# Reordering the setup of a decoupled cross-attention kernel: mask counts, first transposes, image values, output weights and the second batch's keys

## The chip, the cores and the metric

The kernel runs on one core of a Trainium2 chip. The metric is device time in microseconds of one execution; lower is better. Engines are named as in the profile: PE is the matrix engine, PEld its weight loads, DVE the vector engine, ACT the scalar engine, POOL GpSimd, SP the engine that here only issues transfers. A name with q (SPq, ACTq) is an engine's issue of a transfer.

## The reference, cut to what matters

```python
q = split_heads(hidden_states @ w_q, 20)          # hidden_states: 2 x 2048 x 640
k = split_heads(text @ w_k, 20); v = split_heads(text @ w_v, 20)     # text: 2 x 146 x 1024
out_text = merge(sdpa(q, k, v))
mask_ip = ip_mask(bbox, ...)                      # 0 or -10000 for each query and image token
k_ip = split_heads(ip_h @ w_k_ip, 20); v_ip = split_heads(ip_h @ w_v_ip, 20)   # ip_h: 2 x 8 x 1024
out_ip = merge(sdpa(q, k_ip, v_ip, mask=mask_ip))
out = (out_text + out_ip) @ w_out + b_out + residual
```

Each of 20 heads of width 32 attends to 146 text keys and, with a softmax of its own, to 8 image keys.

## The kernel before, in words

Queries are worked in 16 blocks of 256. The first eight belong to batch 0. The work of a block is spread over three stages, of which three neighbouring blocks are in flight at a time: NEXT (X: the transposes of the next block's input), FRONT (Q: query products of five head groups; S: scores with queries on partitions, for their maxima) and BACK (AUX: the maxima transposed; ST: scores with keys on partitions, then the exponentials; PV; AT; O). Each engine walks a list written out by hand (`STEPS`, `ACT_STEPS`, `DVE_STEPS`, `SP_STEPS`), in its order, and waits on counters. Iteration t=0 has FRONT and NEXT only, t=1 is the first with all three.

Every float operand of the large products is split in a high and a low part: ACT copies the high part (`w_high`, `x_high`), DVE subtracts to get the low part (`w_low`, `x_low`), and value units get three parts by `split_values` (first the copy by ACT, then subtract, cast and subtract on DVE).

Before t=0 lies a setup. PE transposes the context, then makes the text keys in five groups (L901), one each as the key weights arrive. Between groups it makes eight "counts" (L913), products of a box indicator with 0/1 weights, which DVE turns into the mask (`mask_values`, L713), four for each batch, through one SBUF tile `mask`. ACT stores a finished half of the mask to DRAM (L572), and DVE's count number 4 waits until the first store has landed. DVE makes the indicator before (L688 to L696) and raises `s_msk` to 3 with it. After the groups come the image keys (L922, bank 7), their rearrangement by a second product (L932, after ACT's `k_ip_rows`), and the transposes of block 0's input (X, L980). The counter `s_klo` reaches 6 when all keys are done. SP then copies batch 0's keys to the stacked operand `k_stack` in 12 issues (`keys_to_stack`, L382), and for each block it copies the queries in two sets to `q_stack` (12 issues each at L457, one of the mask at L460); the first scores wait for both.

Values come in six units (`V_UNITS`, `make_values`): two for batch 0, the 18 remaining text keys of both batches ("rest"), the image tokens ("ip", L960, weights `w_v_ip`), and two for batch 1. They are placed among the steps of t=0 and t=1. Banks 5 to 7 serve them and the key groups; later they are the ST banks. In t=1, before ST(0,2), PE waits for the whole split of all four large units:

```python
if t == 1 and (kind, *args) == ("ST", 0, 2):
    pe.wait_ge(s_vsplit, 4 * V_PARTS)
```

The output weights `wo` are loaded by SP at the end of t=0 and split at five ST steps of t=1 (`W_O_PLACES`; L560 on ACT, L725 on DVE). POOL fills tiles at the start, then casts constant rows into `k_stack` (L490) and copies `v_tail` (L497).

Of the kernel before, what the change touches and what calls it, by code (L numbers as in the profile page):

```python
# [31 lines left out]
F32 = mybir.dt.float32  # L32
# [7 lines left out]
P = 128  # L40
# [28 lines left out]
W_Q_PLACES = {3: (0, 1), 4: (2, 3, 4)}  # L69
# [64 lines left out]
}  # L134
V_COPY_PLACES = {(0, "S", 0, 0, 0): (0, 1), (0, "S", 1, 0, 0): (2,), (0, "S", 1, 1, 0): (3,), (1, "Q", 1): (4,), (1, "ST", 0, 2): (5,)}
V_SPLIT_PLACES = {(0, "S", 0, 0, 0): (0, 1), (1, "S", 4, 0, 0): (4,), (1, "S", 4, 0, 1): (5,)}
W_O_PLACES = {("ST", 2, 0): 0, ("ST", 2, 1): 1, ("ST", 3, 0): 2, ("ST", 3, 1): 3, ("ST", 4, 0): 4}
COUNTS = {0: (0, 3), 1: (3, 4), 3: (4, 7), 4: (7, 8)}
# [83 lines left out]
def attention_kernel(nc, x, ctx, boxes, wq, wk, wv, wk_ip, wv_ip, wo, b_out,  # L222
# [5 lines left out]
    with ExitStack() as stack:  # L228
# [51 lines left out]
        inv_den = sb("inv_den", [P, QT, 8])  # L280
# [82 lines left out]
        def _(sp):  # L363
# [50 lines left out]
            def body(it):  # L414
                t = it.t
                if not it.back:

                    sp.wait_ge(s_klo, GROUPS + 1)

                    sp.wait_ge(stored, 16 * BATCHES)  # L420
                    keys_to_stack(0)
                for stage, kind, args, gen, sc in it.steps(SP_STEPS if it.back else SP_FIRST):
# [10 lines left out]
                    if kind == "XIN":  # L433
# [4 lines left out]
                        if not it.back:  # L438
                            sp.dma_start(w_v_ip, wv_ip.rearrange("(c p) n -> p c n", p=P)).then_inc(s_wv_ip, 16)
# [27 lines left out]
                if not it.back:  # L467
                    before_aux()
# [6 lines left out]
        def _(pool):  # L475
# [6 lines left out]
            nc.gpsimd.memset(k_ip_rows[:], 0.0).then_inc(s_ip_zero, 1)  # L482
            for b in range(BATCHES):
# [48 lines left out]
        def _(act):  # L532
# [29 lines left out]
            for g in range(GROUPS):  # L562
# [4 lines left out]
                                     ACT.Copy, scale=SCALE).then_inc(s_khi, 1)  # L567
                if g in (2, 4):
# [4 lines left out]
                for n in W_Q_PLACES.get(g, ()):  # L573
                    w_high(n)
            act.wait_ge(s_ip_zero, 1)
            act.wait_ge(s_kp, K_IP + 1)
            for j in range(4):
                rows = slice(32 * j, 32 * j + BATCHES * IP)
                nc.scalar.activation(k_ip_rows[rows, :, j, :], k_bank(K_IP)[rows, 0:GROUPS * DH].rearrange("p (g d) -> p g d", d=DH),
                                     ACT.Copy).then_inc(s_ip_rows, 1)  # L580
            act.wait_ge(s_kp, K_IP_T + 1)
            for b in range(BATCHES):
                nc.scalar.activation(k_hi[:, :, b, TEXT:CTX],
                                     k_bank(K_IP_T)[:, 0:GROUPS * BATCHES * IP].rearrange("p (g b k) -> p g b k", g=GROUPS, b=BATCHES)[:, :, b, :],
                                     ACT.Copy, scale=SCALE).then_inc(s_khi, 1)
# [35 lines left out]

            def body(it):
# [47 lines left out]
        def _(dve):  # L670
# [33 lines left out]
            def mask_values(first, end):  # L704

                for n in range(first, end):
# [6 lines left out]
                    nc.vector.tensor_scalar(mask[:, 512 * c:512 * (c + 1)], bank[2 + n % 3][0:IP, :], -1.0, -NEG,  # L713
# [26 lines left out]
            dve.wait_ge(s_khi, GROUPS + BATCHES)  # L740
            for b in range(BATCHES):
                last = nc.vector.scalar_tensor_tensor(
                    out=k_lo[:, :, b, TEXT:CTX],
                    in0=k_bank(K_IP_T)[:, 0:GROUPS * BATCHES * IP].rearrange("p (g b k) -> p g b k", g=GROUPS, b=BATCHES)[:, :, b, :],
                    scalar=SCALE, in1=k_hi[:, :, b, TEXT:CTX].bitcast(F32), op0=ALU.mult, op1=ALU.subtract)
            last.then_inc(s_klo, 1)

# [31 lines left out]

            def body(it):  # L780
# [4 lines left out]
                for stage, kind, args, gen, sc in it.steps(DVE_STEPS):  # L785
                    if isinstance(t, int) and t == 1 and (kind, *args) in W_O_PLACES:
# [86 lines left out]
        def _(pe):  # L873
# [18 lines left out]
            for g in range(GROUPS):  # L892
# [11 lines left out]
                for n in range(*COUNTS.get(g, (0, 0))):  # L904
# [5 lines left out]
                    if n >= 3:  # L910

                        pe.wait_ge(s_mval, n - 2)
                    nc.tensor.matmul(bank[2 + n % 3][0:IP, :], pick[0:9, IP * b:IP * (b + 1)],  # L913
                                     inside[:, 512 * c:512 * (c + 1)], start=True, stop=True).then_inc(s_cnt, 1)

            pe.wait_ge(s_ctx_t, BATCHES + 2)
            pe.wait_ge(s_wk_ip, 16)
            pe.wait_ge(s_klo, 3)
            heads = w_k_ip[:].rearrange("p c (g j d) -> p c g j d", j=4, d=DH)
            for c in range(CC):  # L920
                for j in range(4):
                    last = nc.tensor.matmul(k_bank(K_IP)[32 * j:32 * j + BATCHES * IP, 0:GROUPS * DH],  # L922
# [297 lines left out]
```

## Time and profile before

| | |
|---|---|
| time, median of 3 | 734.93 us (734.69 to 735.64) |
| profiled execution, its own time | 729.49 us |
| its span | 727.7 us |
| PE busy over the span | 688.1 us (95%) |
| DVE, ACT, POOL busy | 74%, 40%, 29% |

The span runs from the first to the last instruction; the execution's own time is 1.8 us longer. Times in rows count from the span's start. In a timeline a row is a run of equal instructions: start, length, engine, line, operation, tiles, and in brackets the engine's idle time before it and what ended it.

### The profile page before, as it was taken

What the parts mean: (1) busy time and instruction counts of PE and PEld (TensorE: products, weight loads), DVE (VectorE), ACT (ScalarE), POOL (GpSimd) and SP (SyncE); (2) the same over time, 40 slices, a digit from 0 to 9 for tenths busy, and PEclk for the clock granted to TensorE, in tenths of its full rate; (3) what the DMA queues carried; (4) which work ended last, traced back from release to release, by engine and by line L of the source; (5) the groups of instructions that cost most, each with busy time, mean ns of one, the idle gap of its engine ahead of it and who ended that gap; (6) DMA issues with size and microseconds to landing.
All of it is one profiled execution on the core that took longest, in us unless ns stands there. A gap on an engine that the chain in (4) does not pass through costs nothing.

```text
span 727.7 us, 18922 instructions
## 1 busy us (share of the span) xinstructions
PE 688.1 (95%) x6410; PEld 628.2 (86%) x6410; DVE 540.1 (74%) x1686; ACT 288.3 (40%) x626; POOL 213.5 (29%) x359
## 2 busy tenths in 40 slices
PE   4979778999999999999999999999999999999987
PEld 3567467989999998989999999999999989899876
DVE  5341539878787979797878788787879797978764
ACT  1031117153534435261617162535444261617061
POOL 7100004324150504142423324151505042423223
PEclk9879999999999999999999999999999999999979
DMA  9935954253434444433435263534344444434310
GB/s 266 323 98 137 267 147 121 66 155 92 136 90 134 102 127 103 140 89 102 130 89 156 68 163 82 147 96 127 98 127 103 133 96 125 104 92 114 90 49 37
DMA packets 79543, 89.52 MB, mean 123 GB/s; under 512 B 10680, under 2 KB 63416, under 8 KB 79492
## 3 DMA queue, kind: packets, MB, share of 16 engines
q1 hardware_dynamic: 79016, 88.45, 44.7%
q10 hardware_dynamic: 492, 0.61, 0.4%
q8 instruction: 21, 0.34, 0.2%
q14 instruction: 14, 0.11, 0.1%
HBM read 39.21 MB, written 10.62 MB: 68 GB/s over the span
## 4 chain that ended last, share of the span: by engine, by line
PE 75%; DMA 8%; DVE 7%; SPq 6%; issue 2%; ACT 1%; ACTq 0%; POOL 0%; DVEq 0%
PE psum L1019 32%; PE psum L1124 9%; PE psum L1076 7%; PE psum L1108 6%; PE psum L1103 5%; DMA q_stack<-aux_a 4%; SPq L457 3%; PE psum L1132 3%; PE psum L901 3%; PE psum L1133 2%; SPq L429 2%; DMA wo_raw<-in_L_xattn_w_v_ip 2%; PE psum L1147 2%; PE psum L980 2%; PE psum L1130 1%
## 5 line engine op out<-in xcount | busy, mean ns | idle before, releaser
L522 POOL TENSOR_TENSOR attn<-o_parts 128x128 f32<-128x128 f32 x160 | 73.8, 461 | 418.9 <-DVE o_parts L844 418.9
L803 DVE TENSOR_REDUCE neg_max<-psum 128x2 f32<-128x292 f32 x320 | 144.7, 452 | 64.0 <-PE psum L1076 63.4
L1019 PE MATMUL psum<-wo_both,at_hi 128*128 128x320 f32 x640 | 153.2, 313 | 0.0
L1019 PE MATMUL psum<-xt_hi,wq_hi 128*128 128x256 f32 x400 | 114.9, 287 | 1.4 <-DVE xt_lo L773 1.4
L1076 PE MATMUL psum<-k_stack,q_stack 104*128 104x154 f32 x640 | 112.6, 286 | 3.5 <-DVE neg_max L804 1.5
L1019 PE MATMUL psum<-xt_hi,wq_lo 128*128 128x256 f32 x400 | 112.1, 280 | 0.0
L1019 PE MATMUL psum<-xt_lo,wq_hi 128*128 128x256 f32 x400 | 112.0, 280 | 0.0
L831 DVE TENSOR_TENSOR p_lo<-psum,p_hi 128x512 f16<-128x512 f32 x160 | 107.9, 682 | 2.8 <-ACT psum L657 2.8
L1019 PEld LDWEIGHTS psum<-wo_both,at_hi 128*128 128x128 f32 x640 | 109.6, 188 | 0.0
L655 ACT ACTIVATE p_hi<-psum 128x512 f16<-128x512 f32 x160 | 95.3, 595 | 27.8 <-PE psum L1103 27.7
L1124 PE MATMUL psum<-v_tail,p_tail 128*128 128x264 f32 x320 | 102.0, 400 | 2.6 <-DVE p_lo L831 1.6
L1076 PEld LDWEIGHTS psum<-k_stack,q_stack 104*128 104x128 f32 x640 | 89.7, 192 | 13.0 <-DVE neg_max L804 9.1
L1019 PE MATMUL psum<-wo_both,at_lo 128*128 128x320 f32 x320 | 98.7, 308 | 0.0
L657 ACT ACTIVATE psum<-psum 128x512 f32<-128x512 f32 x160 | 96.6, 603 | 0.0
L646 ACT ACTIVATE q_hi<-psum 128x256 fp32r<-128x256 f32 x80 | 31.0, 387 | 140.8 <-PE psum L1019 140.8
L527 POOL TENSOR_TENSOR attn<-attn,o_parts 128x128 f32<-128x128 f32 x160 | 74.6, 466 | 12.6
L1019 PEld LDWEIGHTS psum<-xt_hi,wq_hi 128*128 128x128 f32 x400 | 76.7, 192 | 1.7 <-issue 1.7
L1019 PEld LDWEIGHTS psum<-xt_hi,wq_lo 128*128 128x128 f32 x400 | 76.5, 191 | 0.0
L1019 PEld LDWEIGHTS psum<-xt_lo,wq_hi 128*128 128x128 f32 x400 | 76.2, 190 | 0.0
L1132 PEld LDWEIGHTS psum<-v_main,p_hi 128*128 128x128 f16 x640 | 56.6, 97 | 20.3 <-issue 0.3
L844 DVE TENSOR_TENSOR o_parts<-psum,inv_den 128x256 f32<-128x256 f32 x160 | 67.9, 424 | 5.5
L1133 PE MATMUL psum<-v_main,p_lo 128*128 128x65 bf16 x640 | 71.8, 192 | 0.0
(93 smaller groups left out, 1260.3 us busy)
## 6 DMA issues: line engine op xcount, KB each, us to landing
q_stack<-q_hi SPq DMA_DIRECT2D x128, 96.0 KB
x_in<-in_x SPq DMA_DIRECT2D x16, 640.0 KB, 4.1
x_res<-in_x SPq DMA_DIRECT2D x16, 640.0 KB, 5.1
out<-out_sb SPq DMA_DIRECT2D x32, 320.0 KB
q_stack<-q_hi SPq DMA_DIRECT2D x128, 64.0 KB
q_stack<-q_lo SPq DMA_DIRECT2D x64, 96.0 KB
q_stack<-q_lo SPq DMA_DIRECT2D x64, 64.0 KB
q_stack<-aux_a SPq DMA_DIRECT2D x48, 64.0 KB, 2.4
```

The lines of the kernel that those rows point to most:

```text
L522: nc.gpsimd.tensor_tensor(cols, o_parts[:, qt, 0:4, :], o_parts[:, qt, 4:8, :], ALU.add).then_inc(att_half, 1)
L527: nc.gpsimd.tensor_tensor(cols, cols, o_parts[:, qt, 8:12, :], ALU.add).then_inc(att_done, 1)
L655: nc.scalar.activation(p_hi[:, -g % P_SLOTS, 2 * u:2 * u + 2, :].rearrange("p h q -> p (h q)"), src[:], ACT.Exp)
L657: nc.scalar.activation(src[:], src[:], ACT.Exp).then_inc(exp_done, 1)
L803: nc.vector.tensor_reduce(dst[:, :, 0], src[:, :, 0:TEXT], AX_X, ALU.max, negate=True)
L831: nc.vector.tensor_tensor(p_lo[:, -g % P_SLOTS, 2 * u:2 * u + 2, :], scores_t[ST_TURN[(g, u)] % ST_BANKS][:].rearrange("p (h q) -> p h q", ...
L844: nc.vector.tensor_tensor(o_parts[:, qt, 0:8, :], product_1[it.general_bank(gen)][:, :, 0:DH], inv_den[:, qt, :].unsqueeze(2).to_broadcast ...
L1019: last = nc.tensor.matmul(ps, l(c), r(c), start=(i == 0), stop=(i == len(terms) - 1))
L1076: last = nc.tensor.matmul(scores[sc % 2][:, i * CTX:(i + 1) * CTX], q_stack[0:ROW_MAX, h, P * qt:P * (qt + 1)], k_stack[batch][0:ROW_MAX, ...
L1124: nc.tensor.matmul(product_1[it.general_bank(gen)][:, 0:8, :], p_tail[:, -g % P_SLOTS, queries], v_tail[batch][:, g, :].rearrange("p (e d) ...
L1132: nc.tensor.matmul(bank_a[:, VB * j:VB * (j + 1)], hi, values[:, 0:VB], start=False, stop=False)
L1133: last = nc.tensor.matmul(bank_a[:, VB * j:VB * (j + 1)], lo, values[:, 0:VB], start=False, stop=(j == 3))
```

## The change

- The eight counts use two banks (3 and 4) in turn in place of three (2 to 4); they stand after key groups 1, 2 and 3 (3, 2 and 3 of them) in place of groups 0, 1, 3 and 4.
- POOL waits for the indicator (`s_msk` 3) ahead of clearing `k_tail`, and so ahead of its casts.
- PE's order after the groups becomes: X, image keys, image tokens' values, rearranged image keys. ACT and DVE follow. X no longer waits for the mask.
- `w_v_ip` is loaded on SP's queue right behind `wq`, ahead of `wv`; before, it was issued in t=0 behind the first query set and `x_in`.
- The high and low parts of `wq` are made after groups 3 and 4, three and two of them; ACT now does them ahead of the store of the mask.
- `wo` is loaded once batch 0's keys are issued, and split at five S steps of t=0.
- Batch 1's keys go to `k_stack` on ACT's queue, ahead of t=0's first S, in place of SP's queue at the end of t=0. The tails of batch 0's values are issued by SP in t=1, behind the first maxima.
- PE's one wait before ST(0,2) becomes one wait for each of the three banks.
- The SBUF places of `inv_den` and `k_lo` change.

```diff
-W_Q_PLACES = {3: (0, 1), 4: (2, 3, 4)}
+W_Q_PLACES = {3: (0, 1, 2), 4: (3, 4)}
-V_UNITS = [("batch 0", 0, 512), ("batch 0", 512, D), ("rest", 0, D), ("ip", 0, D), ("batch 1", 0, 512), ("batch 1", 512, D)]
+V_UNITS = [("ip", 0, D), ("batch 0", 0, 512), ("batch 0", 512, D), ("rest", 0, D), ("batch 1", 0, 512), ("batch 1", 512, D)]
+V_BANKS = (5, 7, 5, 6, 5, 7)
-W_O_PLACES = {("ST", 2, 0): 0, ("ST", 2, 1): 1, ("ST", 3, 0): 2, ("ST", 3, 1): 3, ("ST", 4, 0): 4}
-COUNTS = {0: (0, 3), 1: (3, 4), 3: (4, 7), 4: (7, 8)}
+W_O_PLACES = {("S", 1, 0, 0): 0, ("S", 1, 0, 1): 1, ("S", 1, 1, 0): 2, ("S", 1, 1, 1): 3, ("S", 2, 0, 0): 4}
+COUNTS = {1: (0, 3), 2: (3, 5), 3: (5, 8)}
...
+        def count_bank(n):
+            return bank[3 + n % 2]
...
             sp.dma_start(wq_raw[:], wq.rearrange("(c p) n -> p c n", p=P)).then_inc(s_wq, 16)
+            sp.dma_start(w_v_ip, wv_ip.rearrange("(c p) n -> p c n", p=P)).then_inc(s_wv_ip, 16)
...
-                    keys_to_stack(0)
+                    keys_to_stack(sp, 0)
+                    sp.wait_ge(s_vp, 1)
+                    sp.dma_start(wo_raw[:, KC:2 * KC, :], wo.rearrange("(c p) n -> p c n", p=P)).then_inc(s_wo, 16)
...
+            pool.wait_ge(s_msk, 3)
             for b in range(BATCHES):
                 nc.gpsimd.memset(k_tail[b][:].bitcast(mybir.dt.uint32), 0).then_inc(s_ktail_zero, 1)
...
+                    if not it.back and (kind, *args) == ("S", 0, 0, 0):
+                        act.wait_ge(s_klo, GROUPS + 1)
+                        act.wait_ge(s_rows, BATCHES)
+                        act.wait_ge(stored, 16 * BATCHES)
+                        keys_to_stack(act, 1)
...
-                    if n >= 3:
-                        pe.wait_ge(s_mval, n - 2)
+                    if n >= 2:
+                        pe.wait_ge(s_mval, n - 1)
...
             pe.wait_ge(x_loaded, 16)
-            pe.wait_ge(s_mval, 2 * 4)
             for u in range(NX):
                 transpose_x(u, general[u])
+            pe.wait_ge(s_ctx_t, BATCHES + 2)
+            pe.wait_ge(s_wk_ip, 16)
+            pe.wait_ge(s_klo, 3)
...
+            make_values(((0, 0, 8),))
+            pe.wait_ge(s_key_pick, 1)
+            pe.wait_ge(s_klo, GROUPS)
+            pe.wait_ge(s_ip_rows, 4)
...
-                        if t == 1 and (kind, *args) == ("ST", 0, 2):
-                            pe.wait_ge(s_vsplit, 4 * V_PARTS)
+                        if t == 1 and kind == "ST" and ST_TURN[args[0], args[1]] < ST_BANKS:
+                            pe.wait_ge(*{5: (s_vsplit, 2 * V_PARTS + 1), 6: (s_vc, 4), 7: (s_vsplit, 3 * V_PARTS + 1)}[
+                                5 + ST_TURN[args[0], args[1]]])
```

## Rows read from the trace of the kernel before

**Rows 1.** Timeline of PE, 19 to 50 us.
```profile
19.86 1.44 PE L913 MATMUL psum<-wo_raw,pick 9*8 9x512 bf16 x3 [5.14 <-DVE wo_raw L696]
21.23 6.19 PE L901 MATMUL psum<-ctx_t,w_kv 128*128 128x292 f32 x16
...
36.45 4.20 PE L901 MATMUL psum<-ctx_t,w_kv 128*128 128x292 f32 x16
...
45.90 2.29 PE L932 MATMUL psum<-key_pick,k_ip_rows 128*128 128x16 f32 x10 [2.64 <-ACT k_ip_rows L579]
48.02 2.37 PE L980 MATMUL psum<-ident,x_in 128*128 128x128 f32 x10
```

**Rows 2.** Timeline of PE, 69 to 108 us: t=0's scores, start of t=1.
```profile
71.88 0.64 PE L1076 MATMUL psum<-k_stack,q_stack 104*128 104x154 f32 x4 [0.71 <-DMA q_stack<-mask_scratch]
...
82.02 2.37 PE L960 MATMUL psum<-wo_raw,rest_t 128*16 128x160 f32 x64 [1.71 <-DMA wo_raw<-in_L_xattn_w_v_ip]
...
88.86 0.39 PE L1086 MATMUL psum<-ident,max_parts_a 128*80 128x128 f32 x2 [1.48 <-issue]
...
106.42 1.49 PE L1108 MATMUL psum<-q_stack,k_tail 120*128 120x256 f32 x8 [3.76 <-DVE v_main L766]
```

**Rows 3.** Timeline of DVE, 0 to 24 us.
```profile
11.12 2.73 DVE L688 TENSOR_SCALAR small<-small 8x32 f32<-8x32 f32 x1
...
16.85 2.96 DVE L696 TENSOR_TENSOR wo_raw<-small 8x2048 bf16<-8x2048 f32 x1
...
20.48 1.87 DVE L713 TENSOR_SCALAR mask<-psum 8x512 f32<-8x512 f32 x3
```

**Rows 4.** Timeline of POOL, 2 to 24 us.
```profile
3.41 4.40 POOL L484 MEMSET k_tail<- 128x2560 uint32 x2
11.04 5.47 POOL L490 CAST k_stack<-row_raw 24x3080 fp32r<-24x3080 f32 x2 [3.23 <-DMA row_raw<-const_stack_rows]
16.57 4.39 POOL L497 COPY v_tail<-v_tail 128x1056 f32<-128x1056 f32 x2
```

**Rows 5.** Chain of work in order of time: start, length, what.
```profile
2.55 6.61 DMA ctx_rest<-in_ctx
```

**Rows 6.** SP's issues at L382, up to 100 us; durations in ns, then landing.
```profile
L382 SPq DMA_DIRECT2D k_stack<-k_hi x16: 585/612/1770, 48.9 to 83.8; - x16
...
DMA to landing us min/median/max: 2.2/4.1/7.6
```

**Rows 7.** Busy time by stretch: PE, PEld, DVE, ACT, POOL; granted clock; DMA share; GB/s.
```profile
45.90:55.80 9.90, 8.54 (x39) 8.17 (x40) 2.01 (x5) 2.15 (x6) 0.00 (x0) 0.50 0.36 76
...
60.00:68.30 8.30, 8.30 (x37) 5.01 (x36) 0.85 (x2) 0.77 (x2) 0.28 (x2) 1.00 0.56 130
106.42:144.47 38.05, 35.71 (x335) 33.13 (x336) 31.38 (x91) 19.43 (x40) 13.99 (x21) 0.96 0.40 107
150.30:183.82 33.52, 33.46 (x335) 31.43 (x336) 27.65 (x88) 16.19 (x35) 12.03 (x21) 1.00 0.42 117
```

**Rows 8.** Timeline of SP's issues, 48 to 70 us.
```profile
48.89 6.00 SPq L382 DMA_DIRECT2D k_stack<-k_hi  x8
54.93 2.56 SPq L382 DMA_DIRECT2D k_stack<-k_lo  x4
...
67.76 0.55 SPq L460 DMA_DIRECT2D q_stack<-mask_scratch  x1
```

**Rows 9.** ACT's timeline, 26 to 46 us.
```profile
36.13 1.36 ACT L555 ACTIVATE wq_hi<-wq_raw 128x640 fp32r<-128x640 f32 x2
```

**Rows 10.** ACT's timeline, 72 to 88 us.
```profile
79.34 0.87 ACT L603 ACTIVATE v_rest<-psum 36x320 f32<-36x320 f32 x2 [4.52 <-PE psum L965]
```

**Rows 11.** The instructions of L725 (min/median/max ns).
```profile
L725 DVE TENSOR_TENSOR wo_both<-wo_raw,wo_both x5: 809/1101/1108, 116.0 to 125.6; 128x640 fp32r<-128x640 f32 x5
```

**Rows 12.** Timeline of DVE, 48 to 125 us: the last value unit's split.
```profile
105.50 0.28 DVE L761 TENSOR_TENSOR v_left<-psum,v_main 128x128 f32<-128x128 f32 x1
...
106.08 0.29 DVE L766 TENSOR_TENSOR v_main<-v_left,v_main 128x128 bf16<-128x128 f32 x1
```

More of the change, by code:

```diff
@@ L270, in attention_kernel @@
         with ExitStack() as setup:
-            k_hi, k_lo = (sb(name, [P, GROUPS, BATCHES, CTX], F32R, setup) for name in ("k_hi", "k_lo"))
+            k_hi = sb("k_hi", [P, GROUPS, BATCHES, CTX], F32R, setup)
             v_left = sb("v_left", [P, 512], where=setup)
+            k_lo = sb("k_lo", [P, GROUPS, BATCHES, CTX], F32R, setup)
             rest_t = sb("rest_t", [P, CC, BATCHES * TAIL], where=setup)
@@ L349, in k_bank, with keys_to_stack @@
         def k_bank(g):
-            return bank[{K_IP: 7, K_IP_T: 5}.get(g, 5 + g % 3)]
+            return bank[{K_IP: 7, K_IP_T: 6}.get(g, 5 + g % 3)]
         def v_bank(n):
-            return bank[5 + n % 3]
+            return bank[V_BANKS[n]]
+        def count_bank(n):
+            return bank[3 + n % 2]
         def column_group(w, g):
             return w.rearrange("(c p) n -> p c n", p=P)[:, :, P * g:P * (g + 1)]
+        def keys_to_stack(queue, b):
+            for row, part in K_PARTS:
+                for j in range(4):
+                    queue.dma_start(k_stack[b][row:row + DH, j:HEADS:4, :].bitcast(F32),
+                                    part[DH * j:DH * (j + 1), :, b, :].bitcast(F32)).then_inc(s_kst[b], 16)
         block = stack.enter_context(nc.Block())
@@ L567, in _ @@
                                      ACT.Copy, scale=SCALE).then_inc(s_khi, 1)
+                for n in W_Q_PLACES.get(g, ()):
+                    w_high(n)
                 if g in (2, 4):
@@ L572, in _ @@
                     act.dma_start(mask_dram[:, b * SEQ:(b + 1) * SEQ], mask[:]).then_inc(stored, 16)
[L573 to L585, printed above, removed]
             def copy_values(units):
@@ L620, in _ @@
                 x_high(u, u + 1, general[u])
+            act.wait_ge(s_ip_zero, 1)
+            act.wait_ge(s_kp, K_IP + 1)
+            for j in range(4):
+                rows = slice(32 * j, 32 * j + BATCHES * IP)
+                nc.scalar.activation(k_ip_rows[rows, :, j, :], k_bank(K_IP)[rows, 0:GROUPS * DH].rearrange("p (g d) -> p g d", d=DH),
+                                     ACT.Copy).then_inc(s_ip_rows, 1)
+            copy_values((0,))
+            act.wait_ge(s_kp, K_IP_T + 1)
+            for b in range(BATCHES):
+                nc.scalar.activation(k_hi[:, :, b, TEXT:CTX],
+                                     k_bank(K_IP_T)[:, 0:GROUPS * BATCHES * IP].rearrange("p (g b k) -> p g b k", g=GROUPS, b=BATCHES)[:, :, b, :],
+                                     ACT.Copy, scale=SCALE).then_inc(s_khi, 1)
             def body(it):
@@ L712, in mask_values @@
                     c = n % 4
-                    nc.vector.tensor_scalar(mask[:, 512 * c:512 * (c + 1)], bank[2 + n % 3][0:IP, :], -1.0, -NEG,
+                    nc.vector.tensor_scalar(mask[:, 512 * c:512 * (c + 1)], count_bank(n)[0:IP, :], -1.0, -NEG,
                                             ALU.max, ALU.mult).then_inc(s_mval, 1)
@@ L739, in _ @@
                     w_low(n)
[L740 to L746, printed above, removed]
             def split_values(units):
@@ L778, in _ @@
                 x_low(u, u + 1, general[u])
+            dve.wait_ge(s_khi, GROUPS + BATCHES)
+            for b in range(BATCHES):
+                last = nc.vector.scalar_tensor_tensor(
+                    out=k_lo[:, :, b, TEXT:CTX],
+                    in0=k_bank(K_IP_T)[:, 0:GROUPS * BATCHES * IP].rearrange("p (g b k) -> p g b k", g=GROUPS, b=BATCHES)[:, :, b, :],
+                    scalar=SCALE, in1=k_hi[:, :, b, TEXT:CTX].bitcast(F32), op0=ALU.mult, op1=ALU.subtract)
+            last.then_inc(s_klo, 1)
             def body(it):
@@ L785, in body @@
                 for stage, kind, args, gen, sc in it.steps(DVE_STEPS):
-                    if isinstance(t, int) and t == 1 and (kind, *args) in W_O_PLACES:
+                    if not it.back and (kind, *args) in W_O_PLACES:
                         w_low(GROUPS + W_O_PLACES[(kind, *args)])
```

71 lines of the change are left out of this document (29 added, 42 removed), and 3 rows, old and new, of the table V_PLACES.

## The prediction, made before the change was run

> **What bounds the kernel now.** I read the page first: PE is busy 95% of the span, and the change leaves the loops over later blocks alone. So only the setup, t=0 and t=1 can give time, and what they give moves everything behind them. Then I read PE's timeline up to the second maxima transposes and asked of each gap what ended it. Before group 1 PE stands 5.14 us until DVE's indicator, and groups after it run slowly: 6.19 us for 16 products that take 4.20 later [rows 1]. Before L932 it stands 2.64 us for ACT's rearrangement, and from there to 55.8 us the granted clock is 0.50, the lower level of 1.2 GHz [rows 1, 7]. In t=0 it stands 1.71 us for `w_v_ip` and 1.48 us for the last maxima, in t=1 3.76 us for the value split [rows 2]. Behind it t=1 takes 38.05 us from ST(0,2) to the next AUX, where t=2 takes 33.52 for the same work [rows 7].
>
> Between setup and t=0 the bound is not PE but SP's issues. They start at 48.89, when the last keys are done (I call that moment K, 48.85). Twelve key issues take 6.00 + 2.56 us, the first query set and its mask end at 68.31, and the first scores start 3.57 us later, at 71.88 [rows 2, 8].
>
> **Indicator and counts.** POOL's two casts (5.47 us for two) and DVE's L688 ran together, and L688, an operation on 8x32, took 2.73 us. L690 did the same [rows 3, 4]. With POOL held back, the indicator loses these waits: it would be ready near 14.5, and group 1 starts right behind group 0, at 14.7 in place of 21.3. Group 1 ends at 18.9. Now the new waits. Count 2 needs a bank that mask 0 frees: ACT's high part 0.41, DVE's low part 0.55, one mask 0.62 (1.87 for three) [rows 3] put it at 20.6, so PE stands 1.3 us. Group 2 ends at 25.1, group 3 at 29.8. Mask 4 waits until the first store has landed, and this store is now issued at 26.9, one group after which DVE wants it; before, there was a whole group between. PE's count 6 waits for mask 4, with group 4 queued behind it; low part 3 and masks 5 to 7 are queued behind it on DVE.
>
> How long does the store take? Small transfers of SP landed in 2.2 to 7.6 us, median 4.1 [rows 6], and one small load in the crowded first ten microseconds took 6.61 [rows 5]. The queue is crowded here too, since 2.6 MB of `w_v_ip` now stand in it. I take 5 us. Then mask 4 is done at 32.5, count 6 runs at 32.6, count 7 waits for mask 5 (33.7), and group 4 starts at 34.0. PE has stood some 3.5 us since 30.0. Gaps of 2.64, 3.76 and 5.14 us were all followed by low clock; I let group 4 take 6.1 us as in [rows 1] and end at 40.1. Before it ended at 40.7: of the 6.6 us won at group 1 nearly all is given back.
>
> **From group 4 to K.** What follows no longer has a gap. X takes 1.2 us (half of 2.37, which was at 0.50), image keys 2.4, image values 2.37 [rows 2], L932 1.2 (half of 2.29), then 0.66 for the last high and low part. `k_ip_rows` (1.24) lies under the image values. Sum 7.8, so K = 47.9, 0.9 earlier than before. With a store of 3 us or less the gap stays short, the clock high, and K = 44.2; with 6.61 it is 49.5.
>
> **From K to the first scores.** Queries are hidden: even at 0.50 three groups are done by K + 8.6, when SP has issued its keys; SP's 2.5 us of idle before the query set vanish. The `wo` issue adds 0.5. So the query set is issued by K + 17.4 and the scores start at K + 21.0, if transfers land as before. They will not quite. The query set alone held 0.56 of the DMA engines [rows 7], so 4.7 us of all of them. Batch 1's keys on ACT's queue, issued in the same stretch, are as much again, and `wo` (1.6 MB, at some 390 GB/s) 4.2 us; that makes 13.5 us of transfers in 8.8 us of issue. Bounds are 0 and 3 us late; I take 2. First scores: 47.9 + 21.0 + 2 = 70.9, against 71.88: **-1.0 us**.
>
> The Trainium skill (DMA: Bandwidth & Descriptors, Issuing engines are not separate DMA queues) says that transfers started by different engines run on the same 16 DMA engines and interleave, and that a second issuer saves only issue time. By that rule the second queue gives SP its time back and no bandwidth; the sum with it is the one above, and without it would be 2 us lower. The share in [rows 7] agrees with counting them as one load.
>
> **t=0.** From the first scores to AUX it took 16.98 us [rows 2]. Image values and the wait for their weights leave: -2.37 - 1.71. Five `w_low` enter DVE's chain: 5 x 0.81 = 4.1 (the 1.10 of others was beside POOL's adds) [rows 11]. The first of them waits for ACT, which copies the "rest" unit (0.87) and makes the first high part (0.68, [rows 9]), while DVE is idle: +1.6 [rows 10]. S(1,0,0) and all S behind it on DVE wait for this, and with them the split of maxima that AUX needs. Sum **+1.5 us**. The issue of batch 1's keys costs ACT 8 us ahead of two value copies; cover is the wait for the query set. Without that cover t=0's value split would wait.
>
> **t=1.** PE now runs the two tail products inside the 3.76 us gap (1.3 us), and the last bank is free at the end of L761, 105.8, not of L766, 106.4: -1.85 [rows 2, 12]. Then the five `w_low` are gone. t=1's excess over t=2 is 38.05 - 33.52 = 4.5 us; its clock was 0.96, and DVE busy 3.7 us more [rows 7]. Moving the subtractions can return most of that, not all, as some gap and some low clock stay. Bounds 2.5 and 4.5; I take 3.9. Sum **-5.7 us**. The later `v_tail` issues (16 of some 0.8 us) end near 102, and PV wants them ten microseconds later: nothing, and if that slack were gone, up to their 7 us.
>
> **Sum.** -1.0 + 1.5 - 5.7 = -5.2 us. The terms come from an execution of 729.49 us, which I take to 724.3. The median of the timed runs is 5.4 us above it; the same difference on it gives 734.9 - 5.2 = **729.7 us**.
>
> **Rivals.** (a) *The store is quick.* It lands within 3 us and the clock stays high: 3.7 less, 726.0. For it the median of 4.1; against it the crowding. (b) *The new wait eats more.* A store of 6.6 us (K = 49.5) and transfers 3 us late: 2.6 more, 732.3. (c) *POOL's casts block DVE at a worse place.* Held back, they run from 18.9 to 24.4 (14.5 + 4.40 + 5.47), just when low part 1 and masks 0 and 1 are due, and PE's count 2 waits for them. If they block as they blocked L688, count 2 runs at 25, 4.4 late, plus up to 1.5 of low clock: 735.5, no change. Against it: the masks at 20.48 ran in 0.62 each while POOL copied until 20.96 [rows 3, 4]; but that was a copy, not a cast. The Trainium skill (SBUF — State Buffer, Who interferes with whom) names the lock: a vector operation with two SBUF inputs contends with a GpSimd one that reads SBUF, one with a single SBUF input outside the two-port modes does not. Low part and mask read PSUM, so by it this rival falls. (d) *The second queue slows the first.* If SP's issues beside ACT's take 1.25 us in place of 0.61, the 13 of the query set take 8.3 us longer: 738.0, slower than before. From 1.0 us each it decides the sign. One issue in [rows 6] took 1.77. Against it: at the start both queues issued together, and ACT's were short. (e) *No gain arrives.* t=0's DVE chain takes what setup and t=1 give, by waits on `wo` too: 734.
>
> **How the numbers follow.** Forecast (5 us store) 0.50, own range 727.5 to 732; (a) 0.17; (b) 0.12; (c) 0.07; (d) 0.08; (e) 0.06. A difference counts from 0.2%, 1.5 us. Faster: forecast, (a), (b) and some of (e), 0.82; same: (c) and the rest of (e), 0.10; slower: (d), 0.08. The range of 725.5 to 734.5 leaves out (c), (d) and a tail of (a).
>
> **What would show it.** The indicator ends near 14.5 and group 1 starts below 15. PE has a gap of some 2.5 us before count 6, ended by mask 4, and DVE one ended by the store. K lies near 48, first scores near 71, AUX near 89.5. The gap before ST(0,2) is under 1.5 us, and no L725 lies in t=1. What would make it wrong: K below 45 or above 51; issues on SP over 1 us; DVE waiting for `wo` or for ACT's value copies in t=0; a gap where nothing in the list has one.

## The result, and the profile after

The changed kernel is slower: 740.06 us median of 9 runs (737.04 to 742.53) against 734.69 (727.83 to 735.64) for the kernel before, ratio 1.0094 with an interval of 1.0062 to 1.0126. The forecast was 729.7, faster. The profiled execution took 742.53 us, its span 740.7.

PE's timeline of the changed kernel (start, length; in brackets the idle time ahead and its end):

```profile
10.96 9.82 PE L909 MATMUL psum<-ctx_t,w_kv 128*128 128x292 f32 x32 [0.61 <-DVE ctx_t L689]
...
34.77 0.37 PE L921 MATMUL psum<-wo_raw,pick 9*8 9x512 bf16 x1 [2.88 <-DVE mask L721]
35.81 0.58 PE L921 MATMUL psum<-wo_raw,pick 9*8 9x512 bf16 x1 [0.66 <-DVE mask L721]
36.32 5.62 PE L909 MATMUL psum<-ctx_t,w_kv 128*128 128x292 f32 x16
...
79.98 1.11 PE L1089 MATMUL psum<-k_stack,q_stack 104*128 104x154 f32 x4 [14.00 <-DMA q_stack<-mask_scratch]
...
93.62 0.53 PE L1089 MATMUL psum<-k_stack,q_stack 104*128 104x154 f32 x2 [2.04 <-DVE neg_max L812]
...
101.65 0.62 PE L1099 MATMUL psum<-ident,max_parts_a 128*80 128x128 f32 x2 [1.48 <-issue]
...
119.37 1.21 PE L1121 MATMUL psum<-q_stack,k_tail 120*128 120x256 f32 x8 [1.00 <-DVE v_left L761]
121.54 0.80 PE L1116 MATMUL psum<-q_stack,k_stack 120*128 120x256 f32 x2 [0.95 <-DVE v_left L761]
```

The row that matters is the fifth of these: the first scores start at 79.98 after 14.00 us of idle PE, where before they started at 71.88 after 0.71 [rows 2]. The setup ahead of it looks as forecast: groups 0 and 1 are one run of 32 products, and the gap is now ahead of counts 6 and 7, ended by the mask. In t=1 the gap of 3.76 us became 1.00 and 0.95.

SP's issues of the changed kernel in the same stretch, and then ACT's:

```profile
49.47 5.30 SPq L369 DMA_DIRECT2D k_stack<-k_hi  x8
54.81 2.56 SPq L369 DMA_DIRECT2D k_stack<-k_lo  x4
57.42 1.28 SPq L423 DMA_DIRECT2D wo_raw<-in_L_xattn_w_out  x1
58.75 2.88 SPq L457 DMA_DIRECT2D q_stack<-q_hi  x4
61.68 3.52 SPq L457 DMA_DIRECT2D q_stack<-q_lo  x4
65.24 3.86 SPq L457 DMA_DIRECT2D q_stack<-q_hi  x4
69.14 0.54 SPq L460 DMA_DIRECT2D q_stack<-mask_scratch  x1
```

```profile
57.45 6.00 ACTq L369 DMA_DIRECT2D k_stack<-k_hi  x8
63.47 4.70 ACTq L369 DMA_DIRECT2D k_stack<-k_lo  x4
```

SP no longer stands between the keys and the query set (it did from 57.5 to 60.0, [rows 8]), but four issues that took 2.54 us before take up to 3.86. The set is all issued at 69.68, 1.4 us later than before. Then comes what weighs most: its last transfer releases PE at 79.98, 10.30 us after its issue; before that was 3.57. The windows of the changed kernel show why (columns as in [rows 7]):

```profile
49.47:57.42 7.95, 7.95 (x71) 7.88 (x70) 1.70 (x4) 1.59 (x5) 0.00 (x0) 1.00 0.59 126
57.42:69.68 12.26, 8.56 (x32) 4.60 (x30) 0.42 (x1) 1.10 (x3) 1.01 (x4) 1.00 1.00 243
69.68:79.98 10.30, 0.00 (x1) 0.03 (x1) 0.00 (x0) 0.00 (x0) 0.28 (x2) 0.51 1.12 195
...
79.98:101.65 21.67, 14.25 (x66) 8.29 (x67) 13.96 (x40) 5.68 (x10) 0.73 (x4) 0.66 0.24 39
101.65:127.04 25.39, 23.43 (x109) 17.51 (x110) 9.05 (x29) 5.60 (x12) 0.00 (x0) 0.77 0.29 79
127.04:157.06 30.02, 29.97 (x304) 27.87 (x303) 24.63 (x78) 12.61 (x27) 12.00 (x21) 0.98 0.35 88
```

From the moment `wo` and batch 1's keys are issued, the 16 DMA engines are full (share 1.00, then 1.12; before it was 0.56, [rows 7]). And PE's granted clock, 1.00 until the gap, is 0.66 over the whole of t=0.

DVE's timeline of the changed kernel, for the setup and the split:

```profile
12.36 2.28 DVE L704 TENSOR_TENSOR wo_raw<-small 8x2048 bf16<-8x2048 f32 x1
21.26 0.52 DVE L740 SCALAR_TENSOR_TENSOR k_lo<-psum,k_hi 128x146 fp32r<-128x146 f32 x2 [3.41 <-ACT k_hi L565]
21.71 1.86 DVE L721 TENSOR_SCALAR mask<-psum 8x512 f32<-8x512 f32 x3
34.04 0.68 DVE L721 TENSOR_SCALAR mask<-psum 8x512 f32<-8x512 f32 x1 [5.51 <-DMA mask_scratch<-mask]
92.29 0.83 DVE L733 TENSOR_TENSOR wo_both<-wo_raw,wo_both 128x640 fp32r<-128x640 f32 x1 [2.59 <-ACT wo_both L560]
```

Below, three marks are taken in each profile: K, SP's first key issue; the first scores; and the first AUX products of t=0, t=1 and t=2.

| profile | K | K to scores | scores to AUX 0 | AUX 0 to 1 | AUX 1 to 2 | AUX 2 at |
|---|---|---|---|---|---|---|
| before | 48.89 | 22.99 | 16.98 | 23.07 | 32.54 | 144.47 |
| after | 49.47 | 30.51 | 21.67 | 25.39 | 30.02 | 157.06 |
| difference | +0.6 | +7.5 | +4.7 | +2.3 | -2.5 | +12.6 |

The spans differ by 13.0 us, so almost nothing comes after AUX 2. The medians differ by 5.4 only: executions of one kernel differ by up to 8 us, and the profile of before was a quick one (729.49). A second profile of before, below, shows where it differs from this one.

### The profile page after: what moved, and what is told of

Its sections match the earlier page's. It is cut to its first block, busy times and chain, and to the rows that moved or that the text cites. A ratio compares the mean times of both kernels' runs of the same rounds, so it can differ in the third digit from the quotient of the medians.

```text
span 740.7 us, 18923 instructions
## 1 busy us (share of the span) xinstructions
PE 692.8 (94%) x6410; PEld 630.3 (85%) x6410; DVE 533.7 (72%) x1686; ACT 288.2 (39%) x626; POOL 209.0 (28%) x359
## 4 chain that ended last, share of the span: by engine, by line
PE 76%; DMA 8%; SPq 7%; DVE 6%; issue 2%; ACT 1%; ACTq 0%; POOL 0%; DVEq 0%
PE psum L1031 31%; PE psum L1137 10%; PE psum L1089 7%; PE psum L1121 6%; PE psum L1116 6%; DMA q_stack<-aux_a 4%; PE psum L1145 3%; PE psum L909 3%; SPq L457 2%; PE psum L1146 2%; SPq L431 2%; DMA x_in<-in_x 2%; PE psum L973 2%; PE psum L1160 2%; PE psum L963 2%
## 5 line engine op out<-in xcount | busy, mean ns | idle before, releaser
L1089 PE MATMUL psum<-k_stack,q_stack 104*128 104x154 f32 x640 | 114.1, 289 | 20.9 <-DMA q_stack<-mask_scratch 14.5
L527 POOL TENSOR_TENSOR attn<-attn,o_parts 128x128 f32<-128x128 f32 x160 | 72.9, 456 | 12.6
```

The costliest lines, as they stand in the source:

```text
L527: nc.gpsimd.tensor_tensor(cols, cols, o_parts[:, qt, 8:12, :], ALU.add).then_inc(att_done, 1)
L1089: last = nc.tensor.matmul(scores[sc % 2][:, i * CTX:(i + 1) * CTX], q_stack[0:ROW_MAX, h, P * qt:P * (qt + 1)], k_stack[batch][0:ROW_MAX, ...
```

## The experiments

Ratios are to runs of the kernel before taken beside them on the same chip; three sets were made, with medians of before of 733.3, 733.8 and 732.1 us.

| run | us | ratio (95%) | K | K to scores | scores to AUX 0 | AUX 0 to 1 | AUX 1 to 2 |
|---|---|---|---|---|---|---|---|
| r0_after | 741.38 | 1.0108 (1.0068 to 1.0148) | 52.24 | 30.47 | 22.42 | 21.60 | 31.47 |
| r1_keys_sp | 736.21 | 1.0034 (1.0008 to 1.0059) | 49.03 | 24.81 | 21.83 | 25.45 | 30.14 |
| r2_wo_late | 730.63 | 0.9971 (0.9950 to 0.9992) | 50.69 | 25.18 | 16.94 | 21.65 | 32.90 |
| r3_both | 728.10 | 0.9937 (0.9905 to 0.9969) | 50.63 | 21.22 | 16.94 | 21.87 | 32.82 |
| r4_mask_tile | 738.64 | 1.0058 (1.0030 to 1.0085) | 45.23 | 29.93 | 21.96 | 21.45 | 31.53 |
| r5_rest_early | 725.44 | 0.9898 (0.9866 to 0.9931) | 50.82 | 21.42 | 12.30 | 22.48 | 33.57 |
| r7_wo_gap | 725.39 | 0.9883 (0.9855 to 0.9912) | 50.39 | 20.75 | 16.73 | 21.82 | 31.67 |
| r8_filler | 728.27 | 0.9918 (0.9888 to 0.9948) | 50.46 | 21.19 | 16.20 | 21.85 | 34.86 |
| r9_before | 733.34 | 1.0012 (0.9982 to 1.0043) | 50.20 | 23.75 | 16.86 | 26.97 | 32.63 |
| r6_tails | 727.57 | 0.9928 (0.9905 to 0.9952) | 50.66 | 21.03 | 16.64 | 21.68 | 33.72 |
| r10_combined | 721.75 | 0.9863 (0.9827 to 0.9899) | 48.74 | 21.19 | 12.34 | 22.55 | 29.83 |
| r11_comb_mask | 718.33 | 0.9813 (0.9777 to 0.9849) | 46.79 | 20.87 | 12.33 | 25.26 | 30.07 |

### Which load delays the first scores: r0 to r3

r0_after is the changed kernel again, without an edit.

> The changed kernel once more, on the chip of the three runs beside it, as their base. All theories: some 740 us, the first scores near 80 us, 10 us after SP's last issue of the query set.

r1_keys_sp gives batch 1's keys back to SP at the end of t=0:

```diff
-                    if not it.back and (kind, *args) == ("S", 0, 0, 0):
-                        ...
-                        keys_to_stack(act, 1)
...
+                if not it.back:
+                    keys_to_stack(sp, 1)
```

> Batch 1's keys go back to SP's queue at the end of t=0; all else as changed. Theory 1 (the query set of the first scores lands late because batch 1's keys and wo share the DMA engines with it, each by its own transfer time): some 5 us of transfers leave the stretch, first scores near 75, time 3 to 5 us below the changed kernel. Theory 2 (the second queue is what hurts, as the engines serve two queues in turn, and wo would be nearly harmless): first scores near 71, 8 or 9 us below. Theory 3 (wo alone): no change.

r2_wo_late gives `wo` back instead: loaded at the end of t=0, split in t=1.

```diff
-W_O_PLACES = {("S", 1, 0, 0): 0, ("S", 1, 0, 1): 1, ("S", 1, 1, 0): 2, ("S", 1, 1, 1): 3, ("S", 2, 0, 0): 4}
+W_O_PLACES = {("ST", 2, 0): 0, ("ST", 2, 1): 1, ("ST", 3, 0): 2, ("ST", 3, 1): 3, ("ST", 4, 0): 4}
...
                     keys_to_stack(sp, 0)
-                    sp.wait_ge(s_vp, 1)
-                    sp.dma_start(wo_raw[:, KC:2 * KC, :], wo.rearrange("(c p) n -> p c n", p=P)).then_inc(s_wo, 16)
...
+                if not it.back:
+                    sp.wait_ge(s_vp, 1)
+                    sp.dma_start(wo_raw[:, KC:2 * KC, :], wo.rearrange("(c p) n -> p c n", p=P)).then_inc(s_wo, 16)
```

> wo is loaded at the end of SP's t=0 and split in t=1, as before; batch 1's keys stay on ACT's queue. Theory 1: some 4 us of transfers leave, first scores near 76; t=0 loses its five subtractions (some 5 us shorter), t=1 gains them; time 3 to 4 us below the changed kernel. Theory 2: first scores near 79, the time within 1 us of the changed kernel. Theory 3 (wo alone makes the set late): first scores near 71.

r3_both makes both edits.

> Both moved back. All three theories: the query set lands within 4 us of its last issue, first scores at 70 to 71. If the rest of the forecast holds (bank by bank waits give 2 us, t=0 loses 4 us of image values), the time is 3 to 6 us under the kernel before; if not, something else in the setup's order costs time too.

The first scores came at 73.84, 75.87 and 71.85: Theory 1 comes near all three (75, 76, and 70 to 71), Theories 2 and 3 do not. The times fit it less well: for r2, 3 to 4 us below the changed kernel were expected and 10.8 came (below).

Windows from K to the first scores, for r3_both, r1_keys_sp and r2_wo_late, one fence each (the last columns are the granted clock, the DMA share and GB/s; the first row is the stretch after the last issue of the query set, the second the whole):

```profile
68.06:71.85 3.79, 0.00 (x1) 0.03 (x1) 0.00 (x0) 0.00 (x0) 0.00 (x0) 1.00 0.70 174
50.63:71.85 21.22, 16.51 (x103) 12.52 (x101) 2.12 (x5) 2.81 (x7) 1.01 (x4) 1.00 0.61 139
```

```profile
68.23:73.84 5.61, 0.00 (x1) 0.03 (x1) 0.00 (x0) 0.00 (x0) 0.00 (x0) 0.75 1.08 185
49.03:73.84 24.81, 16.84 (x103) 12.84 (x101) 2.12 (x5) 2.81 (x7) 1.01 (x4) 0.94 0.85 188
```

```profile
70.29:75.87 5.58, 0.00 (x1) 0.03 (x1) 0.00 (x0) 0.00 (x0) 1.01 (x4) 0.68 1.09 179
50.69:75.87 25.18, 16.84 (x103) 12.85 (x101) 2.12 (x5) 2.69 (x7) 2.02 (x8) 0.93 0.87 166
```

With neither load, K to scores takes 21.22 us. `wo` alone adds 3.6, batch 1's keys alone add 4.0, both add 9.3 (30.51 and 30.47 in two executions). Together they cost 1.7 us more than the sum of the two alone. One profile each stands behind r1 and r2, but the stretch hardly varies between executions: 20.75 to 21.42 us in the seven profiles without either load behind K, 29.93 to 30.51 in the three with both. Share times length gives the time of all DMA engines: 12.9 us with neither, 21.1 with `wo`, 21.9 with the keys, 28.4 with both (0.93 x 30.51). The extra transfers took the engines 8 to 9 us each, not the 4.2 and 4.7 of the prediction; a packet may take longer among others (the share passes 1 while few GB/s move), but no run shows that by itself. Of 8.2 us that `wo` adds 3.6 appear as delay, of the keys' 9.0 us 4.0, of the 15.5 of both 9.3. The rest (4.6, 5.0, 6.2) must have gone where the engines were idle, 8.3 us of this stretch in r3. Two loads cannot both have the same idle time, which would explain the 1.7 us; that is a reading of these sums, not tested by a run.

The issues are slowed as well. By what, the runs leave open. SP's timeline of r2_wo_late, where ACT issues beside SP and `wo` is not loaded:

```profile
58.62 3.67 SPq L454 DMA_DIRECT2D q_stack<-q_hi  x4
62.34 3.64 SPq L454 DMA_DIRECT2D q_stack<-q_lo  x4
66.02 3.17 SPq L454 DMA_DIRECT2D q_stack<-q_hi  x4
```

and of r1_keys_sp, where ACT issues nothing beside SP:

```profile
58.87 2.52 SPq L457 DMA_DIRECT2D q_stack<-q_hi  x4
61.43 3.63 SPq L457 DMA_DIRECT2D q_stack<-q_lo  x4
65.11 2.54 SPq L457 DMA_DIRECT2D q_stack<-q_hi  x4
```

With ACT issuing, all three groups of four are slow, the first at a DMA share of only 0.69. Without it, one of three is (a single issue of 1.45 us in it), while the other two take their usual 2.52 and 2.54 at shares of 0.91 and 1.14. So full DMA engines alone do not explain the slow issues, and ACT's issuing is not cleared of them. In time, taking the keys off ACT's queue is worth 5.2 us (741.38 to 736.21), taking `wo` away 10.8, both 13.3; `wo` weighs more since its split leaves t=0 with it (scores to AUX 0: 22.42 and 21.83 with it, 16.94 twice without), and AUX 1 to 2 in r2 takes back only 1.4 of these 5.5 us.

### The mask's one tile: r4

r4_mask_tile gives batch 1's mask rows of its own, so mask 4 has no store to wait for.

```diff
-            mask = sb("mask", [IP, SEQ], where=setup)
+            mask = sb("mask", [32 + IP, SEQ], where=setup)
...
-                    if n == 4:
-                        dve.wait_ge(stored, 16)
```

> The changed kernel, but the second batch's mask has rows of its own in the mask tile, so that DVE's mask 4 no longer waits for the first store. Theory A (the store wait cost the setup what I worked out, 3 us of gap and up to 3 of low clock, and SP's start sets the first scores): keys done 4 to 6 us earlier, near 44 to 46, first scores near 75, time 4 to 6 us below the changed kernel. Theory B (by then the DMA engines set the first scores, not the start of SP's issues): keys earlier all the same, first scores less so, the time 0 to 3 us below.

PE's timeline of r4_mask_tile:

```profile
33.19 0.37 PE L918 MATMUL psum<-wo_raw,pick 9*8 9x512 bf16 x1 [1.25 <-DVE mask L718]
33.50 4.20 PE L906 MATMUL psum<-ctx_t,w_kv 128*128 128x292 f32 x16
...
75.16 1.10 PE L1086 MATMUL psum<-k_stack,q_stack 104*128 104x154 f32 x4 [13.41 <-DMA q_stack<-mask_scratch]
```

The gap shrinks from 2.88 + 0.66 to 1.25 us, so the store was its cause, and group 4 behind it takes 4.20 us, not 5.62. K comes at 45.23, 4.2 us earlier than after and 7.0 earlier than r0 (K in the profiles of the new order with the wait lies between 48.74 and 52.24). The first scores follow, at 75.16, as Theory A said: they stay 29.93 us behind K, so SP's start still counts beside full engines. The time gained is less than Theory A's 4 to 6 us, 2.7 us from r0, and the intervals of the two ratios overlap. Beside the two loads PE still stands 13.41 us ahead of the first scores. In r11, where neither load is issued behind K, the medians with and without this edit differ by 3.4 us (721.75 and 718.33; these intervals overlap too), and K by 1.95.

### What t=0 lost: r5, r7, r8

All three start from r3 or r1. r5_rest_early moves the "rest" unit whole ahead of the first scores, into the gap:

```diff
-    (0, "S", 0, 0, 0): ((1, 0, 8), (2, 0, 8)), (0, "S", 0, 1, 0): ((3, 0, 4),), (0, "S", 1, 0, 0): ((3, 4, 8),),
+    (0, "S", 0, 0, 0): ((1, 0, 8), (2, 0, 8), (3, 0, 8)),
...
-V_COPY_PLACES = {(0, "S", 0, 0, 0): (1, 2), (0, "S", 1, 0, 0): (3,), (1, "Q", 1): (4,), (1, "ST", 0, 2): (5,)}
+V_COPY_PLACES = {(0, "S", 0, 0, 0): (1, 2, 3), (1, "Q", 1): (4,), (1, "ST", 0, 2): (5,)}
```

> On top of the run with both moved back: PE makes the 'rest' unit of values (4.6 us at full clock) ahead of the first scores too, where it stood 4.7 us. Theory C (a gap ahead of the first scores lowers PE's clock, and t=0 then pays half speed on top of work that could have lain in the gap): t=0 from first scores to AUX falls from 16.9 to some 9 to 11 us, time 6 to 8 us below that run. Theory D (DVE and x_in bound t=0, PE has slack): t=0 falls by no more than 3 us.

r7_wo_gap (on r1) loads `wo` ahead of the wait for K, at 48.48 where r1 did at 58.23, and splits it whole before the first scores:

```diff
+                    sp.wait_ge(s_vp, 1)
+                    sp.dma_start(wo_raw[:, KC:2 * KC, :], wo.rearrange("(c p) n -> p c n", p=P)).then_inc(s_wo, 16)
                     sp.wait_ge(s_klo, GROUPS + 1)
...
-W_O_PLACES = {("S", 1, 0, 0): 0, ("S", 1, 0, 1): 1, ("S", 1, 1, 0): 2, ("S", 1, 1, 1): 3, ("S", 2, 0, 0): 4}
+W_O_PLACES = {("S", 0, 0, 0): (0, 1, 2, 3, 4)}
```

> Batch 1's keys on SP as before; wo is loaded ahead of batch 0's keys and split on ACT and DVE ahead of the first S, where both stood idle for over 10 us. Theory 1 (transfers beside the query set make it late): wo is gone from that stretch, first scores at 70 to 72 as with both moved back. t=0 has no subtractions, t=1 neither, so t=1 from its second AUX to the next AUX takes 30.1 us in place of 32.8: 2 to 3 us below the run with both moved back. If wo now makes batch 0's keys late enough to hold the first scores, it is 2 to 4 us more.

r8_filler (on r3) lets PE do the "rest" products once more in the gap, into bank 6, where the real ones later overwrite them; it adds 4.5 us of PE work and nothing else.

```diff
+                            for c in range(CC):
+                                for half in range(2):
+                                    nc.tensor.matmul(bank[6][64 * half:64 * half + BATCHES * REM, 0:2 * GROUPS * DH],
+                                                     rest_t[:, c, 0:BATCHES * REM], filler[:, c, :, half, :],
+                                                     start=c == 0, stop=c == CC - 1)
```

> The run with both moved back, and in PE's gap ahead of the first scores the 'rest' products once more, into a bank whose result is overwritten by the real ones; it adds 4.6 us of PE work and takes nothing away. Theory C (the gap lowers the clock): the granted clock stays at 1.00 from the first scores on, the 'rest' products take 2.35 us a half in place of 4, and the time falls by 2 to 4 us although there is more work. Theory D: the same or slower.

PE's timelines of r3_both, r8_filler and r5_rest_early, in this order:

```profile
71.85 0.75 PE L1084 MATMUL psum<-k_stack,q_stack 104*128 104x154 f32 x4 [4.71 <-DMA q_stack<-mask_scratch]
...
75.13 4.28 PE L953 MATMUL psum<-w_kv,rest_t 128*36 128x320 f32 x16
...
79.94 2.35 PE L953 MATMUL psum<-w_kv,rest_t 128*36 128x320 f32 x16
```

```profile
67.22 4.50 PE L1052 MATMUL psum<-w_kv,rest_t 128*36 128x320 f32 x32
71.65 0.67 PE L1090 MATMUL psum<-k_stack,q_stack 104*128 104x154 f32 x4
73.85 0.66 PE L968 MATMUL psum<-ident,x_in 128*128 128x128 f32 x4 [1.52 <-DMA x_in<-in_x]
74.44 4.04 PE L953 MATMUL psum<-w_kv,rest_t 128*36 128x320 f32 x16
```

```profile
67.58 4.50 PE L953 MATMUL psum<-w_kv,rest_t 128*36 128x320 f32 x32
72.24 0.65 PE L1084 MATMUL psum<-k_stack,q_stack 104*128 104x154 f32 x4 [0.16 <-DMA q_stack<-mask_scratch]
```

In r3 equal runs of 16 products take 4.28 us soon after the gap and 2.35 a little later: the lower of the clock's two levels, 1.2 GHz, then the upper. The filler closes the gap, but the x_in wait of 1.52 us stays and the products behind it take 4.04, so Theory C's "stays at 1.00" failed (0.80 over t=0, against 0.71 in r3). Scores to AUX 0 goes from 16.94 to 16.20, the time from 728.10 to 728.27, which is no difference. So the gap ahead of the scores alone is not what sets the clock of t=0. The second profile of the kernel before says the same. It has the short gap of 0.71 us and 0.81 us of wait for x_in, and still:

```profile
75.40 0.66 PE L980 MATMUL psum<-ident,x_in 128*128 128x128 f32 x4 [0.81 <-DMA x_in<-in_x]
75.99 4.04 PE L965 MATMUL psum<-w_kv,rest_t 128*36 128x320 f32 x16
```

In its first profile these 16 took 2.35 behind waits of 0.71 and 0.95. So a slow start of t=0 belongs in part to the execution and not to the change. Moving the real work into the gap pays: 12.30 us in t=0, 4.6 less than in r3 (9 to 11 were expected), though the clock fell there as well. The time is 725.44, 2.7 below r3 where 6 to 8 were expected, and the intervals of the two ratios overlap. Splitting `wo` in the gap (r7) leaves t=0 at 16.73, where the split among the S steps made it 21.83, and keeps it out of t=1 too: 725.39 us against 736.21 for r1. The same load costs the first scores nothing there: K to scores takes 20.75 us, though the DMA share over it is 0.92. Issued 9.8 us later, in r1, it cost 3.6. By these two runs, what delays the query set is not how much is loaded between K and the scores, but what is still under way beside the set itself.

### The tails, and the kernel before again: r6, r9

r6_tails (on r3) issues the tails of batch 0's values at the end of t=0, ahead of t=1, as before:

```diff
-                sp.wait_ge(s_ones_all, BATCHES)
-                sp.wait_ge(s_vc, 4)
-                fill_tails(0)
...
+                    sp.wait_ge(s_ones_all, BATCHES)
+                    sp.wait_ge(s_vc, 4)
+                    fill_tails(0)
```

> The run with both moved back, and SP issues the tails of batch 0's values at the end of t=0 again. Theory E (those eight issues push the loads of x_in and x_res against the second maxima, so that PE waits 1.3 us for aux_b): x_in is issued 6 us earlier, the wait for aux_b goes, t=1 is 1 to 2 us shorter. Theory F (aux_b is late for another reason): no change.

PE's timeline of r2_wo_late shows the wait in question, which r0, r3, r4, r5, r7 and r8 have too (1.63, 1.31, 1.69, 1.98, 1.78 and 2.90 us):

```profile
120.85 0.50 PE L1116 MATMUL psum<-q_stack,k_stack 120*128 120x256 f32 x2 [1.39 <-DMA q_stack<-aux_b]
```

With the tails moved it is gone, as Theory E said, but t=1 is no shorter (AUX 1 to 2 takes 33.72 us, in r3 32.82), and the time is 727.57 against 728.10 for r3, in another set of runs: no difference that can be told.

r9_before is the kernel before, without an edit.

> The kernel before, profiled once more: its first profile (729.49 us) is among the quickest of its executions, whose times spread over 8 us. All theories take the same stages (keys done near 49, first scores near 72, second AUX near 144.5); what differs in this profile shows where its executions differ.

Its windows, by the same marks as [rows 2]'s stretches (first scores to AUX 0, to AUX 1, to AUX 2):

```profile
73.95:90.81 16.86, 14.12 (x131) 8.27 (x131) 10.58 (x35) 3.63 (x9) 0.00 (x0) 0.87 1.11 281
90.81:117.78 26.97, 23.21 (x109) 17.54 (x110) 9.05 (x29) 5.61 (x12) 1.02 (x4) 0.77 0.51 143
117.78:150.41 32.63, 30.37 (x305) 27.78 (x304) 28.80 (x83) 15.51 (x32) 13.98 (x21) 1.00 0.33 81
```

Its span is 734.5 us, 6.8 more than the first profile of the same kernel, and 3.9 of that lie between AUX 0 and AUX 1, where the clock was 0.77 and in the first profile 0.93. Most of the difference between these two thus lies in one stretch, where the clock was lower; two profiles do not say it of all executions. Against this profile the changed kernel stands at -0.7 (K), +6.8, +4.8, -1.6 and -2.6, together +6.7 us at AUX 2, close to the 5.4 between the medians.

### Together: r10 and r11

r10_combined puts the edits of r7, r5 and r6 on the changed kernel; r11_comb_mask adds that of r4.

> Together: batch 1's keys on SP, wo loaded ahead of batch 0's keys and split ahead of the first S, the 'rest' unit ahead of the first scores, tails of batch 0 as before. If the gains are of different stages they add: 721 to 723 us, 1.5 to 1.8% below the kernel before. If DVE and x_in bound t=0 whatever PE does, no better than the best so far, 725.

> The same and rows of its own for the second mask. Keys done near 45.5 in place of 50; since nothing now holds the query set's transfers, all of it should reach the first scores: 4 to 5 us below the run beside it, 717 to 719 us. If the DMA engines and not SP's start set the first scores, 0 to 2 us.

721.75 and 718.33 us: the last is 1.9% faster than the kernel before (0.9777 to 0.9849) and by the two ratios 3% faster than the change as made. Both times lie in the expected ranges, but r11 is 3.4 us below r10 where 4 to 5 were expected. It has no new work, only other places: K at 46.79, scores 20.87 us behind it, t=0 in 12.33.

## Why the prediction was wrong

**The step that failed is "From K to the first scores."** It took K + 21.0 for the issue and landing, and 2 us for the loads beside it, with bounds of 0 and 3. The base was right: with neither load r3 needs 21.22. The added term was 9.3 us, not 2, and 7.3 us more alone turn -5.2 into +2.1. The other terms missed too. In the order K, K to scores, t=0, t=1 the misses are 1.5, 7.6, 3.2 and 5.5 us against the first profile of before, and 0.2, 6.9, 3.3 and 1.5 against r9_before; this step is the largest in both. The step had counted 13.5 us of transfers in 8.8 us of issue, which is 4.7 over, and then bounded the delay at 3 without a row. Even 4.7 would have been half of the 9.3. The larger fault is the price: the two loads were put at 8.9 us of all engines, by a share of 0.56 and a rate of 390 GB/s from stretches without such a mix, and took 15.5 (28.4 less 12.9). What r1 to r3 show in its place: each load delays the scores by 3.6 to 4.0 us alone, and both by 9.3. The forecast was right that the second queue brings no bandwidth of its own: with the keys on it, and `wo` away, the set came 4.0 us late.

**K.** Forecast 47.9, measured 49.47 and 52.24 (and 45.23 without the store's wait). The steps happened as told: DVE's L704 ends at 14.64, group 1 follows without a gap, PE stands 2.88 + 0.66 us before the last counts, DVE 5.51 for the store, which was issued at 28.56 and released mask 4 at 34.04, some 5.5 us (5 was taken). What came on top is the time of groups 0 and 1, 9.82 us for 32 products where I had 4.2 for each 16. With it all behind came later: the store was issued at 28.56 and not 26.9, and group 4 ended at 41.94, not 40.1. From there to K it took 7.5 us where 7.8 was forecast. So of the 6.6 us won at group 1 nothing reached K. In r0 these 32 products took 10.61 us and group 4 took 7.23, in r10 8.13 and 6.86: 2.9 of the 3.5 us between these two K lie in the length of these products.

**t=0, +1.5.** Measured +4.7. The cost of the splits was sized right: 5.7 forecast, 4.9 measured (21.83 in r1, 16.94 in r3). The relief was not: without the image values and without the splits t=0 still takes 16.94, as before. PE's busy time there is 13.13 us in r3 where 12.44 less 2.37, that is 10.1, were to be left; the granted clock was 0.71 against 1.00. The step assumed the upper level in t=0. It was not given even where the gap ahead of the scores was filled (r8) or as short as before (r9_before, clock 0.87), so the gap that the change opens there (4.71 us in r3, 14.00 after) is at most a part of the cause. The other relief, the 1.71 us of wait for `w_v_ip`, is absent in r9_before as well: with slower products ahead, PE comes to them after the weights.

**t=1, -5.7.** The bank waits came to 1.95 in place of 3.76, -1.8 as forecast. The subtractions were worth less: AUX 1 to AUX 2 takes 29.83 to 31.67 in the seven profiles without them (after, r0, r1, r4, r7, r10, r11), and 32.54 to 34.86 in the seven with them. Most pairs differ by 1 to 3 us, around the lower bound of 2.5 and not 3.9. In the profiles of after, r1 and r11 part of it was lost again between AUX 0 and 1, which took 25.3 to 25.5 us at a clock of 0.77 where r0 took 21.60; so they differ less over both stretches together. From AUX 0 to AUX 2 the first profile of before took 55.61 us, after 55.41 and r0 53.07, and r9_before 59.60: by the first profile the term of -5.7 was nearly all missed, by the second it is mostly there. That the later `v_tail` issues cost nothing missed waits of 1.3 to 2.9 us for `aux_b`, of no visible worth in time.

**The rivals.** (d), the one on the slower side, gave 738.0: its sign was right and its mechanism half. SP's 13 issues of the query set took 10.9 us in place of 8.3, 2.7 more and not 8.3 more; the rest was the landing, which (d) did not have. Single issues did pass 1 us (1.34 to 1.59 in r0), one of the signs named beforehand. Against (d) stood that at the start ACT's issues beside SP's were short. It left out the other side: there SP's five issues of key weights took 10.40 us, 2.08 each. (c) falls: POOL's casts ran from 19.24 to 24.69, and beside them two of L740 took 0.52 us and three masks 1.86, as without. (a) and (b) turned on the store, which took 5.5 us. (e) named DVE's chain in t=0, and r1 against r3 shows it at 4.9 us, but not as what decided.

**What stays open.** Whether the idle time used twice over is why both loads together cost 1.7 us more than their sum; what slows the issues; why the clock falls in some executions and not in others in the first groups and between AUX 0 and 1; and what in t=0 makes it fall even with the gap ahead of the scores filled (r8).

## What to carry to other kernels

Before a load is moved to an earlier place, look at which transfer ends a wait in that stretch, and whether the load will still be under way beside it, on whichever queue it is issued: `wo` cost the first scores 3.6 us when issued just ahead of the query set and nothing when issued 9.8 us earlier. Count the idle time of the DMA engines once for all added loads, and do not price a load in a crowd by what it took alone (8.9 us forecast, 15.5 measured). Give idle engines the work instead: the "rest" products ahead of the scores took 4.6 us out of t=0 (r3 to r5), and the splits of `wo` moved ahead of them 5.1 (r1 to r7). And where a sum gives a number (4.7 us over), a smaller bound beside it needs a row of its own.

## What the runs showed of the hardware

- Full DMA engines: with small-row copies among them (from the set's last issue to the first scores) the share read 1.08 to 1.13 while only 179 to 195 GB/s moved; the page of the profile shows 390 GB/s for its second slice (18.5 to 37 us), the weights' loads. A transfer that was waited for 3.8 us after its issue took 5.6 with either load beside it and 9.0 to 10.3 with both.
- Four issues on SP that took 2.54 us took 2.88 to 4.78 in the three profiles with both loads; four on ACT took 4.70 in after (median of one 1.28). At a DMA share of 1.14 and no issues on ACT, four on SP still took 2.54 (r1).
- Equal runs of 16 products took 4.28 us soon after a gap of 4.71 us and 2.35 five microseconds later (r3). In the kernel before, the first of them took 2.35 us in one profile and 4.04 in another, behind gaps of under 1 us in both.
- One kernel's executions spread over 8 us (727.83 to 735.64), and of the 6.8 between two profiles 3.9 lie in one stretch with 0.77 in place of 0.93 of the clock.
